# Attention one: gathers, shifts, layer-norm statistics and transpositions at other banks of a pass

## What is computed

```python
h = _L0_tok_ref(x, L0_tok_W)                       # W.T[tokens]
h = h + _L0_attn_ref(_layernorm(h, axis=-1), ...)  # attention one: 16 heads of 16
h = h + _L0_ffn_ref(_layernorm(h, axis=-1), ...)   # four experts, the top two
h = h + _L1_attn_ref(_layernorm(h, axis=-1), ...)  # attention two
h = h + _L1_ffn_ref(_layernorm(h, axis=-1), ...)   # FP4 linear layers
```

```python
qkv = jnp.einsum('bhce,ef->bhcf', xh, Wqkv) + bqkv
q, k, v = jnp.split(qkv, 3, axis=-1)
att = jnp.einsum('bhqe,bhke->bhqk', q, k) / jnp.sqrt(jnp.float32(he))
mask = jnp.tril(jnp.ones((c, c), dtype=att.dtype), k=-1)
att = jax.nn.softmax(att * mask, axis=-1)
out = jnp.einsum('bhqk,bhke->bhqe', att, v)
out = out.transpose(0, 2, 1, 3).reshape(b, c, d)
out = out @ Wr + br
```

## Time and profile before

| | us |
|---|---|
| median of 3 runs | 2953.96 (2953.74 to 2954.68) |
| the profiled execution | 2954.28 |
| its span from first to last instruction | 2952.5 |
| granted TensorE clock, mean of the span | 0.94 of full speed |
| PE / DVE / ACT / POOL busy | 2543.3 / 2114.0 / 1509.7 / 1644.1 |

### The profile page before, as it was taken

The page is one execution under the profiler, slowest core; times in us unless marked ns, Lnnn a source line. Parts: engine busy times, 40 slices in busy tenths (PEclk is TensorE's granted clock), DMA queues, the critical chain, the costliest instruction groups (busy, mean ns, idle before and its releaser), DMA issues. The chain is left out here.

```text
span 2952.5 us, 58168 instructions
## 1 busy us (share of the span) xinstructions
PE 2543.3 (86%) x15254; PEld 1489.2 (50%) x15318; DVE 2114.0 (72%) x5668; ACT 1509.7 (51%) x3246; POOL 1644.1 (56%) x2564
## 2 busy tenths in 40 slices
PE   1768888888888888888876999999999979999999
PEld 0323433333443333443354666666666647666676
DVE  2656667766666776766646999999999865565554
ACT  1335555555555555555532655565555544444444
POOL 3663343433343433343244878888877757776775
PEclk7679999999999999999977999999999979999999
DMA  3343433443443443443340000000000000000000
GB/s 57 92 111 58 64 57 51 64 71 51 64 60 54 57 72 54 61 64 52 58 139 0 1 1 0 0 0 0 0 0 0 1 4 17 14 16 14 16 16 18
DMA packets 81255, 112.93 MB, mean 38 GB/s; under 512 B 25101, under 2 KB 37145, under 8 KB 80537
## 3 DMA queue, kind: packets, MB, share of 16 engines
q1 hardware_dynamic: 76360, 101.44, 20.1%
q0 software_dynamic: 3072, 8.39, 1.0%
q10 hardware_dynamic: 1744, 2.16, 0.2%
HBM read 18.98 MB, written 8.39 MB: 9 GB/s over the span
## 5 line engine op out<-in xcount | busy, mean ns | idle before, releaser
L661 DVE TENSOR_REDUCE cand<-ring 128x4 f32<-128x512 f32 x1152 | 713.5, 681 | 389.4 <-PE ring L771 369.8
L570 ACT ACTIVATE probs<-scoresT 128x512 f32<-128x512 f32 x1152 | 624.4, 605 | 624.9 <-PE scoresT L715 622.3
L491 POOL TENSOR_SCALAR_AFFINE_SELECT probs<-probs 128x256 f32<-128x256 f32 x512 | 204.8, 414 | 464.9 <-ACT probs L570 458.2
L715 PE MATMUL scoresT<-stage 98*128 98x512 bf16 (+3 forms) x1536 | 381.6, 340 | 41.8 <-ACT probs L570 28.0
L735 PE MATMUL pv<-probs,Vg 128*32 128x512 f32 (+3 forms) x3072 | 344.6, 573 | 23.8 <-POOL probs L491 18.0
L771 PE MATMUL ring<-Km,Qm 64*128 64x512 bf16 (+2 forms) x1792 | 230.3, 323 | 95.8 <-DVE cand L661 44.5
L1198 PE MATMUL mm<-w_W,hT 128*128 128x256 f32 x1024 | 243.2, 381 | 8.0 <-ACT z L1286 3.3
L1218 PE MATMUL mm<-w_W,x2T 128*128 128x512 f32 x512 | 242.7, 597 | 0.3 <-DVE x L1437 0.2
L715 PEld LDWEIGHTS scoresT<-stage 98*128 98x128 bf16 x1536 | 122.1, 99 | 219.3 <-ACT probs L570 126.6
L771 PEld LDWEIGHTS ring<-Km,Qm 64*128 64x128 bf16 x1792 | 76.5, 96 | 295.7 <-issue 120.1
L1279 ACT ACTIVATE hT<-mmT,w_be,w_g 128x128 f32<-128x128 f32 x512 | 185.5, 468 | 78.1 <-PE mmT L1209 78.1
(11 more groups left out here) (254 smaller groups left out, 5270.0 us busy)
## 6 DMA issues: line engine op xcount, KB each, us to landing
stage<-parts SPq DMA_DIRECT2D x256, 96.0 KB, 2.8
stage<-parts SPq DMA_DIRECT2D x256, 64.0 KB, 2.8
Qm<-parts SPq DMA_DIRECT2D x128, 128.0 KB, 2.6
Km<-parts SPq DMA_DIRECT2D x128, 128.0 KB, 2.7
stage<-parts SPq DMA_DIRECT2D x256, 32.0 KB, 2.4
out<-result SPq DMA_DIRECT2D x64, 128.0 KB, 1.7
stage<-ct SPq DMA_DIRECT2D x128, 4.0 KB
w_W<-in_W SPq DMA_DIRECT2D x4, 512.0 KB
```

Source lines behind the costliest of these rows:

```text
L491: nc.gpsimd.affine_select(out=d, in_=d, compare_op=ALU.is_gt, fill=0.0, base=0, pattern=[[0, 2], [1, P]], channel_multiplier=-1).then_inc( ...
L570: nc.scalar.activation(probs[:, buffer(slot), :], scoresT[slot % SCORE_BANKS][:], ACT.Exp, scale=SOFT).then_inc(exp_ok, 1)
L661: ins = nc.vector.tensor_reduce(c, src[:].rearrange("p (t a b) -> p t a b", t=c.shape[1], b=P), AX.X, ALU.max)
L715: ins = nc.tensor.matmul(scoresT[slot % SCORE_BANKS][:, at:at + hi - lo], Ks[0:ROWS, gi, hh, P * kt:P * kt + P], Qs[0:ROWS, gi, hh, lo:hi] ...
```

## The change

Six tables and rules of the order are changed; nothing that is computed.

- XT moves from banks 4 and 7 to 6 and 8, the first QK from 9 to 10.
- `LN_STATS` moves from banks 20, 23, 25, 28 of an odd pass to 12, 15, 18, 21.
- Burst 3 and the last MX position move from bank 30 to 29.
- Burst 4 of the pass before moves from bank 0 to bank 1, behind the first four MX banks and the second bank of scores.
- GpSimd's three instructions of a shift are now an event of their own, `SHIFT`: for the first pair of heads at bank 18 and not 15, for the second at bank 33 and not 30, behind the masks of banks 31 to 33.
- The 56 gathers stand two by two behind banks 0 to 27 of the first even pass; none is left in the first odd pass.

```diff
-BURST_AT = {0: 11, 1: 15, 2: 22, 3: 30}
-
-MAX_AT = (0, 3, 7, 11, 15, 18, 22, 26, 30)
+BURST_AT = {0: 11, 1: 15, 2: 22, 3: 29}
...
-    0: {"LN_NORM": (1, 2, 4, 5), "XT": (4, 7), ... "QK": (9, 13, 17, 20), ...
-    1: {"LN_STATS": (20, 23, 25, 28), "PV_COPY": 4, ...
+    0: {"LN_NORM": (1, 2, 4, 5), "XT": (6, 8), ... "QK": (10, 13, 17, 20), ...
+    1: {"LN_STATS": (12, 15, 18, 21), "PV_COPY": 4, ...
...
+MAX_AT = (0, 3, 7, 11, 15, 18, 22, 26, 29)
+SHIFT_LAST = 33
...
     if tail:
-        at(0, ("PV", -1, 4))
+        at(1 if scores else 0, ("PV", -1, 4))
...
         for n, u in enumerate(uses):
             at(MAX_AT[n // 2] if scores else pos_of["MX"] + n, *u)
+            if n % MAX_BANKS == 2 and n > MAX_BANKS:
+                at(MAX_AT[n // 2] if scores else pos_of["MX"] + n, ("SHIFT", 0))
+        at(SHIFT_LAST, ("SHIFT", PAIRS_MX - 1))
...
-                            if section == "first" and gi * UNITS + slot < TILES - TPB:
-                                gather(TPB + gi * UNITS + slot, gat1)
+                            if section == "first" and gi == 0 and 2 * slot < TILES - TPB:
+                                gather(TPB + 2 * slot, gat1)
+                                gather(TPB + 2 * slot + 1, gat1)
...
-                        elif kind == "MAX_FINAL":
+                        elif kind == "SHIFT":
```

More of the change, by code:

```diff
@@ L142 @@
 AT = {
-    0: {"LN_NORM": (1, 2, 4, 5), "XT": (4, 7), "PV_COPY": 4, "EQ": 6, "TMP": 0, "PT": 5, "OT": 24, "WR": 25, "RSUM": 3, "SUF": 12, "QK": (9, 13, 17, 20), "MID_LAG": 2, "V": 21, "VG": 5, "LOAD": 0, "PV_HALF": 17},
-    1: {"LN_STATS": (20, 23, 25, 28), "PV_COPY": 4, "EQ": 6, "TMP": 0, "PT": 5, "WR": 2, "V": 8, "VG": 6, "LOAD": 0, "PV_HALF": 17},
+    0: {"LN_NORM": (1, 2, 4, 5), "XT": (6, 8), "PV_COPY": 4, "EQ": 6, "TMP": 0, "PT": 5, "OT": 24, "WR": 25, "RSUM": 3, "SUF": 12, "QK": (10, 13, 17, 20), "MID_LAG": 2, "V": 21, "VG": 5, "LOAD": 0, "PV_HALF": 17},
+    1: {"LN_STATS": (12, 15, 18, 21), "PV_COPY": 4, "EQ": 6, "TMP": 0, "PT": 5, "WR": 2, "V": 8, "VG": 6, "LOAD": 0, "PV_HALF": 17},
     "V_IN": 0, "WR_IN": 1,
 }
+MAX_AT = (0, 3, 7, 11, 15, 18, 22, 26, 29)
+SHIFT_LAST = 33
 ALONE = {"LN_STATS": (0, 0, 0, 0), "LN_NORM": (1, 1, 1, 1), "XT": (2, 2), "QK": (8, 9, 10, 11), "MID_LAG": 1, "V": 12, "PV_COPY": 1, "TMP": 2, "PT": 5, "OT": 11,
```

## The result

The changed kernel takes 2975.12 us (median of 4 runs, 2969.74 to 2977.07), the kernel before 2954.32 beside it (2953.74 to 2954.96). The ratio is 1.0067, interval 1.005 to 1.0085: 0.7% slower. I had forecast 2938.5 with a range up to 2960; sign and range are both missed.

A forecast was written before the change was run, and what follows sets the result against it. TensorE, busy 2543.3 of 2952.5 us, was taken to bound the kernel. Loop pairs -34.5, last halves -3.7, first half +14 and clock +8.5 gave -15.7 from 2954.3: forecast 2938.5, range 2920 to 2960.

The forecast's parts named there:

- The gathers: First half: 26 extra gathers of 1.25 us delay bank 27's mask to 178.8; odd pass gives 14.7 back; net +14.
- the five named places: TensorE's waits: none ahead of burst 4 or XT, 1.5 and 0.8 at bank 7, 1.5 and 1.2 at bank 18, 1.2 for `c`.
- 1.2 and 0.2 at CT: Pass ends: CT comes 1.2 us earlier in 13 odd passes, 0.2 earlier in 15 even ones.
- Burst 4: Pass start: MX and bank 1 cover the 0.77 mask wait and leave half clock; -1.65 odd pass, -0.1 even.
- The first step that failed: Even pass: XT two banks later; its 1.52 wait goes, waits at bank 7 come; net -0.65 us at the first QK.
- The row on `xn`: VectorE: four `xn` take 1.64 us beside the sums of `Rsum`, 1.10 without; +0.5 booked against XT's move.
- Statistics: Odd pass, bank 18: two parts ahead of the maxima make TensorE's ring-bank waits of 0.41 and 1.16 grow by 1.15.
- The second step that failed: Even pass, bank 7: clock falls in half of 13 passes at 1.3 us each, +8.5.
- rival (2): Slower: clock falls at bank 7 in all 13 even passes, stays down a second stretch at bank 18; 2963.5; chance 0.14.
- the last halves: Last two halves, without statistics: about -1.65 for burst 4 and -0.2 for CT each, one the -0.65; booked as -3.7.
- rival (4): Loop gains half the forecast (low bounds of CT and burst 4), same first half: 2953, no change; chance 0.18.
- The reason I gave against the fall at bank 7: For rival (1): at the 1.52 wait ahead of XT the granted clock stayed at 1.00, from 1002.2 to 1046.5.

The follow-up runs named there:

- the base: The changed kernel with the old gathers, one behind each bank over both first-half passes, and first-half statistics at 20 to 28: 2958.17 us, ratio 1.0017.
- the fastest one: The changed kernel with old gathers, XT and QK back, loop statistics at 9, 12, 21, 21 (2915.25 us), plus repeated matmuls in remaining waits: 2859.05, ratio 0.9688.

## Why the prediction was wrong

**The gathers: right.** +14 forecast, +16.3 measured, +15 with nothing else changed. The chain (26 extra gathers of 1.25, the mask at 178.8) holds within a microsecond. What was short is what the odd pass gives back: TensorE comes out of 10.18 us of idleness, and burst 4 then takes 3.21, at half clock; I had taken the loop's odd pass, where burst 4 takes 2.84 and would leave the slow stretch with the change.

**The waits of the loop: right at the five named places, too hopeful in sum.** By my terms TensorE's idle time should fall by 1.7 a pair (1.2 and 0.2 at CT, 0.77 at burst 4, 0.65 at XT, less 1.15 for the statistics); it fell by 0.9, and by 1.0 in the mean of the loop. CT of an odd pass now waits 1.08 where it had waited 1.64, of an even pass 1.08 for 0.99.

**Burst 4: mechanism right, size too small.** -1.75 a pair was forecast; the run with this line alone shows -2.24, with a wait 2.3 shorter, since it also takes away most of XT's.

**The first step that failed: XT's move, wrong sign.** The -0.65 took the removal of XT's wait as its gain, which burst 4's line gives without it. Alone the move costs 9 us, and undone in the base it gains 19, or 1.6 a pair. The waits that I forecast in its place (1.5 and 0.8) are its real effect. The row on `xn` that I weighed against it holds: four `xn` take 1.76 beside the sums and 1.11 without them (VectorE, the changed kernel):

```profile
1023.62 1.11 DVE L643 TENSOR_SCALAR xn<-h,mv,rstd 128x128 f32 x4
...
1029.70 1.76 DVE L643 TENSOR_SCALAR xn<-h,mv,rstd 128x128 f32 x4
```

**Statistics: size right, consequence missed.** The waits at bank 18 grew by 1.1 as forecast. But the clock already fell behind them, and in the changed kernel it now stays down for 6.9 and not 3.4. The length of the waits alone doesn't decide that: with the same 2.68 the statistics alone show 6.8 in half of the pairs, and TensorE's busy time doesn't rise.

**The second step that failed: the clock.** I booked half of 13 falls at bank 7, 8.5 us, and left the three old stretches as they were. What came is the mechanism of rival (2): a fall at bank 7 in 12 of the 13 even passes and a second stretch at bank 18; and one thing that no case held, a second stretch behind the end of the odd pass, against the one that went at the start of the odd pass. TensorE's busy time rose by 1.5 a pair where I had it fall by 0.35: that is the clock's part, 1.85 a pair or some 24 us. The waits fell by 0.7 less than my terms had it, some 9 us, and XT's move is the term of them whose sign was wrong. Together these are 33 of the 36.6 us by which the forecast was off; the first half makes 2.3 of the rest. The two parts can't be had one by one, since XT's move also brings the fall at bank 7, and moving the statistics away from bank 18 takes 1.9 of busy time back from the base.

Rival (2) had a chance of 0.14; its 2963.5 is nearer than the forecast, with the falls right in kind, and my range ended above the forecast but below it. Part of that nearness is luck: it priced each further stretch at 1.3 us, where the two that came net cost 0.7 each, and kept XT's gain. Two slips of the sums are small beside this: the last halves leave out the 0.65 that the text gives one of them, and rival (4) reaches 2953 only without the 8.5 for the clock. The reason I gave against the fall at bank 7 (the clock had stayed up behind a wait of 1.52) was read from one place; at bank 7 two waits of 2.4 in sum stand close together. Which difference between the two places counts, no run isolates.

The Trainium skill (TensorE: Matmul & The Clock Gate, "Part 1: The HAM clock gate") takes the penalty of the ramp at half clock to be under 1% of a typical kernel's span. It says so of the warm-up. In this kernel the clock falls again in every pair, and the measurement decides what that costs: filling waits of about 1.0 to 1.6 us gave 1.3% in the kernel before and 1.9% in the fastest one (2915.25 to 2859.05).

**What stays open.** Why pairs settle at 88.7 or 85.3 us, and why the four parts alone give 42 us and together none, is not shown. I take it that where a stretch of half clock falls depends on the waits before it and on the falls before those; the two patterns of the shift alone fit that. I can't compute it from the trace of before.

## What to carry to other kernels

Where TensorE falls to half clock behind short waits, look at the granted clock first and cost each wait twice: its own length, and some 0.2 to 0.5 us for each microsecond that the clock then stands at half. A wait that can't be removed may be filled: matmuls repeated into a bank that nobody has read yet took 1.3% off the kernel before and 1.9% off the best order. When two edits could each end the same wait, try each alone before both are taken, since here one gave all of the gain and the other only moved the wait. And where the runs of one kernel fall into two groups, look at its pairs one by one before its median is compared with anything.

## What the runs showed of the hardware

- In the kernel before and the changed one, TensorE's granted clock fell to 1.2 GHz behind waits of 1.6 to 2.7 us in sum, the longest single one of 1.0 to 1.8, each time for 3.4 or 6.8 us. 16 matmuls of 512 columns then take 3.2 to 3.6 us instead of 1.7 to 1.9.
- 7 us more of half clock in a pair (10 to 17) made TensorE's busy time 1.46 us longer, 0.2 us per microsecond; 10 us more in the same kernel (shift alone, 3.5 to 13.6) made it 3.9 longer, 0.4 per microsecond, as in a dense burst (1.28 of 3.20 us, 1.93 of 3.64).
- Pairs of eight kernels settled at one of two lengths, 88.7 or 85.3 us. Adding 0.86 us of work to a pair left its length at 88.76; taking 1.0 us of waiting from it (the statistics at 9, 12, 21, 21) shortened it by 2.8.
- Indirect gathers cost GpSimd 1.25 us each when they follow one another (0.95 and 0.30 of issue); 27 more of them ahead of a mask put it 32 us later.
